# Attention kernel: the third chunk of 64 dimensions computed in full 128-row and 128-column matmul shapes

## What is computed

```python
# layer 0
q = heads(x @ W_q); k_t, v_t = heads(text @ W_k), heads(text @ W_v)        # 1020 text tokens
probs_t = softmax(q @ k_t.T * scale); text_out = probs_t @ v_t
k_ip, v_ip = heads(ip @ W_k_ip), heads(ip @ W_v_ip)                        # the last 4 tokens
sem = l2norm(probs_t @ text) @ l2norm(ip).T
ip_out = (softmax(q @ k_ip.T * scale + 0.5 * sem) * mask) @ v_ip
x = (text_out + ip_out) @ W_out + b_out + x
# layer 1: 77 text tokens and 947 ip tokens, each with its own softmax
q = split(x @ Wq.T); out = attend(q, text @ Wk.T, text @ Wv.T) + attend(q, ip @ Wk_ip.T, ip @ Wv_ip.T)
x = out @ Wo.T + bo + x
```

## Time and profile before

| | |
|---|---|
| three timed runs | 3520.0, 3520.13, 3522.02 us; median 3520.13 us |
| the profiled execution | span 3517.6 us, from first to last instruction; the profile gives no other time of it |
| PE | busy 3406.7 us, 97% of the span, 24832 matmuls |
| PEld | busy 2900.3 us, 82% |
| DVE | busy 2044.4 us, 58% |
| ACT | busy 1845.3 us, 52% |
| POOL | busy 1095.2 us, 31% |
| granted TensorE clock | 0.990 of 2.4 GHz on the mean |

### The profile page before, as it was taken

The page is one execution under the profiler, slowest core; times in us unless marked ns, Lnnn a source line. Parts: engine busy times, 40 slices in busy tenths (PEclk is TensorE's granted clock), DMA queues, the critical chain, the costliest instruction groups (busy, mean ns, idle before and its releaser), DMA issues.

```text
span 3517.6 us, 65886 instructions
## 1 busy us (share of the span) xinstructions
PE 3406.7 (97%) x24832; PEld 2900.3 (82%) x24832; DVE 2044.4 (58%) x5565; ACT 1845.3 (52%) x4030; POOL 1095.2 (31%) x932
## 2 busy tenths in 40 slices
PE   6999999999999999999999999999999999999978
PEld 4888978887888888888888878888788888889755
DVE  4444445556555565665656556656566656565678
ACT  2333333556454555555655555555555556565757
POOL 2111010234332332233333232333423322222467
PEclk8999999999999999999999999999999999999989
DMA  5433822233348333233356423324335532222233
GB/s 183 107 77 64 104 82 74 70 88 83 82 83 76 93 75 83 76 100 84 94 76 71 97 71 76 80 74 107 86 74 78 69 61 62 55 55 53 52 78 64
DMA packets 659087, 282.78 MB, mean 80 GB/s; under 512 B 481010, under 2 KB 609730, under 8 KB 658772
## 3 DMA queue, kind: packets, MB, share of 16 engines
q1 hardware_dynamic: 658772, 278.57, 38.2%
HBM read 199.44 MB, written 79.04 MB: 79 GB/s over the span
## 4 chain that ended last, share of the span: by engine, by line
PE 88%; DVE 6%; ACT 2%; issue 1%; POOL 1%; SPq 1%; DMA 1%; POOLq 0%; DVEq 0%; ACTq 0%
PE acc L1095 9%; PE acc L1088 9%; PE acc L1090 8%; PE acc L1091 8%; PE acc L1096 8%; PE acc L1089 7%; PE score L1055 4%; PE score L1139 4%; PE spare L1139 4%; PE score L1057 3%; PE av L1126 3%; PE av L1130 3%; PE score L1176 2%; PE spare L1176 2%; PE score L1225 2%; PE spare L1225 2%
## 5 line engine op out<-in xcount | busy, mean ns | idle before, releaser
L1298 ACT ACTIVATE prob<-score 128x512 f32<-128x512 f32 x1219 | 729.3, 598 | 1252.5 <-PE score L1057 1244.4
L1698 POOL TENSOR_TENSOR prob_lo<-prob,prob_hi 128x512 fp32r<-128x512 f32 x624 | 816.1, 1312 | 1525.5 <-ACT prob_hi L1301 1524.9
L1088 PE MATMUL acc<-tok_v,prob_hi 128*128 128x300 f32 x2240 | 904.1, 404 | 0.9 <-issue 0.9
L1090 PE MATMUL acc<-tok_lo,prob_hi 128*128 128x256 f32 (+1 forms) x2560 | 755.5, 295 | 0.0
L1095 PE MATMUL acc<-tok_v,prob_lo 128*128 128x278 f32 (+1 forms) x2560 | 745.8, 291 | 0.0
L1301 ACT ACTIVATE prob_hi<-score 128x512 fp32r<-128x512 f32 x1219 | 726.0, 596 | 0.0
L1091 PE MATMUL acc<-tok_lo,prob_hi 128*128 128x256 f32 (+1 forms) x2560 | 719.5, 281 | 0.0
L1096 PE MATMUL acc<-tok_v,prob_lo 128*128 128x256 f32 (+1 forms) x2560 | 717.7, 280 | 0.0
L1089 PE MATMUL acc<-tok_v,prob_hi 128*128 128x256 f32 x2240 | 627.4, 280 | 0.0
L1090 PEld LDWEIGHTS acc<-tok_lo,prob_hi 128*128 128x128 f32 (+1 forms) x2560 | 484.2, 189 | 9.1 <-issue 7.2
L1091 PEld LDWEIGHTS acc<-tok_lo,prob_hi 128*128 128x128 f32 (+1 forms) x2560 | 483.6, 189 | 6.3 <-issue 1.0
(11 more groups left out here) (325 smaller groups left out, 5141.1 us busy)
## 6 DMA issues: line engine op xcount, KB each, us to landing
k_ring<-k_scr SPq DMA_DIRECT2D x160, 384.0 KB
tok_v<-v_scr SPq DMA_DIRECT2D x158, 176.0 KB, 3.3
v_ring<-v_scr SPq DMA_DIRECT2D x160, 148.5 KB, 3.4
ctx_t<-in_ctxT SPq DMA_DIRECT2D x16, 1024.0 KB, 9.1
q_ring<-q_scr SPq DMA_DIRECT2D x160, 96.0 KB
v_scr<-v_stage SPq DMA_DIRECT2D x32, 440.0 KB, 2.6
v_scr<-v_stage SPq DMA_DIRECT2D x36, 330.0 KB, 9.6
tok_stage<-in_ctx SPq DMA_DIRECT2D x32, 256.0 KB, 2.9
```

The source lines that it names most:

```text
L1088: e.matmul(out_a[:, 0:SEG + VCOLS], p_hi, tok_v[0:kk, c, seg, v_lo:v_lo + SEG + VCOLS], start=first, stop=False)
L1090: e.matmul(out_a[:, t0:t0 + SEG], p_hi, tok_lo[0:kk, c, seg * SEG:(seg + 1) * SEG], start=False, stop=False)
L1298: e.activation(prob[:, es, :], bank_s[:, :], ACT.Exp, scale=SCALE)
L1698: e.tensor_tensor(prob_lo[:, ps, :], prob[:, es, :], prob_hi.bitcast(F32)[:, ps, :], ALU.subtract).then_inc(s_low[1], 1)
```

## The change

In all four places the third chunk is computed at full size.
- The four operands of the two projections, `w_q`, `x_in`, `w_o` and `o_t`, get 64 rows of zeros in their third chunk, written once at the start by eight memsets at the head of DVE's program. All query and finish matmuls then contract over 128 rows. Their number of columns stays `MW[m]`.
- Keys and turns of m = 2 use the last 128 output channels (192 to 319) as columns in place of the last 64. The wanted 64 channels then stand in PSUM rows 64 to 127, the other rows repeat channels of m = 1 and are not used.
- So for m = 2 the turned rows are copied from and into rows 64 to 127, `w_o`'s third chunk is loaded there, and its zeros lie in rows 0 to 63. The keys are split on all 128 rows and stored from rows 64 to 127. `edge` is as before.
- PE waits for the zeros ahead of the first query and the first finish step (`s_pad`).

```diff
+        s_pad = sem("unused_rows_zeroed")
+        HALF = P - MW[NM - 1]
+        low_rows, high_rows = slice(0, MW[NM - 1]), slice(HALF, P)
+        def rows_of_chunks(name, x):
+            return [x[:, 0:NM - 1, :], x[high_rows if name == "wo" else low_rows, NM - 1, :]]
+        def columns_to_rows(m):
+            return slice(P * m, P * m + P) if m < NM - 1 else slice(D - P, D)
+        def rows_in_psum(m):
+            return slice(0, P) if m < NM - 1 else high_rows
+        def rows_of_split(key):
+            return slice(0, P if key[0] == "k" else MW[key[2]])
...
 # PE, q
+                            if u == 0:
+                                e.wait_ge(s_pad, 4)
-  mm = e.matmul(bank[bank_of["q", u, m]][0:w, 0:SQ], w_q[wj][0:MW[k], k, P * m:P * m + w], x_in[xj][0:MW[k], k, :],
+  mm = e.matmul(bank[bank_of["q", u, m]][0:w, 0:SQ], w_q[wj][:, k, P * m:P * m + w], x_in[xj][:, k, :],
 # PE, k
-  mm = e.matmul(bank[bank_of[key]][0:w, lo:hi], (w_ip if layer else w_text)[:, k, P * m:P * m + w], ctx_t[:, k, t0 + lo:t0 + hi],
+  mm = e.matmul(bank[bank_of[key]][:, lo:hi], (w_ip if layer else w_text)[:, k, columns_to_rows(m)], ctx_t[:, k, t0 + lo:t0 + hi],
 # PE, turn
-  fl = [attn[:, st, :, :].rearrange("p h d -> p (h d)")[:, P * m:P * m + w] for st in range(ST)]
+  fl = [attn[:, st, :, :].rearrange("p h d -> p (h d)")[:, cols] for st in range(ST)]
-  e.matmul(bg[0:w, 0:SQ], v_block[:, batch_of(u) % 2, P * m:P * m + w], probs_t, start=True, stop=True)
+  e.matmul(bg[:, 0:SQ], v_block[:, batch_of(u) % 2, cols], probs_t, start=True, stop=True)
-  mm = e.matmul(bg[0:w, st * P:(st + 1) * P], fl[st], ident[:], start=False, stop=True, skip_group_check=True)
+  mm = e.matmul(bg[:, st * P:(st + 1) * P], fl[st], ident[:], start=False, stop=True, skip_group_check=True)
 # PE, finish
+                        if u == 0:
+                            e.wait_ge(s_pad, 8)
-  mm = e.matmul(bank[bank_of[key]][0:w, 0:SQ], w_o[wj][0:MW[k], k, P * m:P * m + w], o_t[oj][0:MW[k], k, :],
+  mm = e.matmul(bank[bank_of[key]][0:w, 0:SQ], w_o[wj][:, k, P * m:P * m + w], o_t[oj][:, k, :],
 # DVE, ahead of all steps
+            for x in (*w_q, *x_in):
+                e.memset(x.bitcast(F32)[high_rows, NM - 1, :], 0.0).then_inc(s_pad, 1)
+            for x in (*w_o, *o_t):
+                e.memset(x.bitcast(F32)[low_rows, NM - 1, :], 0.0).then_inc(s_pad, 1)
...
 # DVE, turn
+  w, key = rows_in_psum(m), ("turn", u, m)
-  e.tensor_copy(o_t[0][0:w, m, :], turned).then_inc(s_turned, 1)
+  e.tensor_copy(o_t[0][w, m, :], turned).then_inc(s_turned, 1)
 # DVE, split (split_hi and lower in the same way, on DVE and POOL)
-  e.tensor_copy(f, bank[bank_of[key]][0:w, lo:hi]).then_inc(s_free, 1)
+  w, (lo, hi) = rows_of_split(key), columns_of(key)
+  e.tensor_copy(f, bank[bank_of[key]][w, lo:hi]).then_inc(s_free, 1)
 # SP
-  e.dma_start(w_o_raw[0:MW[m], m, :], a[f"wo{UNITS[u][0]}"][P * m:P * m + MW[m], :]).then_inc(s_wo, 16)
+  e.dma_start(w_o_raw[rows_in_psum(m), m, :], a[f"wo{UNITS[u][0]}"][P * m:P * m + MW[m], :]).then_inc(s_wo, 16)
+  w = rows_in_psum(m) if key[0] == "k" else slice(0, n_rows)
-  part_bf[0:w, i % 2, 0:hi - lo, c0:c1]).then_inc(s_part[i % 2], 16)
+  part_bf[w, i % 2, 0:hi - lo, c0:c1]).then_inc(s_part[i % 2], 16)
```

More of the change, by code:

```diff
@@ L1166, in _ @@
                     _, u, m, half, k = s
-                    layer, w, t0 = UNITS[u][0], MW[m], 512 * half
+                    layer, t0 = UNITS[u][0], 512 * half
                     key = ("k", u, m, half)
@@ L1330, in _ @@
                         e.wait_ge(s_bg, note[s] + 1)
-                    for h, f in zip(rows_of_chunks(hi), rows_of_chunks(raw)):
+                    for h, f in zip(rows_of_chunks(name, hi), rows_of_chunks(name, raw)):
                         e.activation(h, f, ACT.Copy).then_inc(s_hi[name], 1)
@@ L1405, in _ @@
                     _, u, m, key, i = s
-                    w, (lo, hi) = MW[m], columns_of(key)
-                    f = part_f[0:w, i % 2, lo:hi]
+                    w, (lo, hi) = rows_of_split(key), columns_of(key)
+                    f = part_f[w, i % 2, lo:hi]
                     e.wait_ge(s_bg, job[key] + 1)
@@ L1410, in _ @@
                         e.wait_ge(s_part[i % 2], part_waits[i])
[L1411 removed]
+                    e.tensor_copy(f, bank[bank_of[key]][w, lo:hi]).then_inc(s_free, 1)
                 elif kind == "split_hi":
                     _, u, m, key, i = s
[L1414 removed]
+                    w, (lo, hi) = rows_of_split(key), columns_of(key)
                     e.wait_ge(*out_of_psum[job[key]])
[L1416 removed]
+                    e.tensor_copy(part_bf[w, i % 2, 0, lo:hi], part_f[w, i % 2, lo:hi]).then_inc(s_h0, 1)
                 elif kind == "lower":
                     _, u, m, key, i = s
[L1419 removed]
+                    w, (lo, hi) = rows_of_split(key), columns_of(key)
                     e.wait_ge(s_r, i + 1)
[L1421 removed]
+                    e.tensor_copy(part_bf[w, i % 2, 1, lo:hi], part_r[w, i % 2, lo:hi]).then_inc(s_h1, 1)
                 elif kind == "ip_squares":
@@ L1669, in _ @@
                     e.wait_ge(s_hi[name], 2 * nth_of[u] + i + 1)
-                    e.tensor_tensor(rows_of_chunks(lo)[i], rows_of_chunks(raw)[i], rows_of_chunks(hi.bitcast(F32))[i], ALU.subtract).then_inc(s_lo[name], 1)
+                    e.tensor_tensor(rows_of_chunks(name, lo)[i], rows_of_chunks(name, raw)[i], rows_of_chunks(name, hi.bitcast(F32))[i], ALU.subtract).then_inc(s_lo[name], 1)
                 elif kind == "turn" and s[3] == (ST if UNITS[s[1]][0] == 0 else 0):
                     _, u, m, _ = s
-                    w, key = MW[m], ("turn", u, m)
+                    w, key = rows_in_psum(m), ("turn", u, m)
                     e.wait_ge(s_bg, job[key] + 1)
-                    turned = bank[bank_of[key]][0:w, 0:SQ]
-                    e.tensor_copy(o_t[0][0:w, m, :], turned).then_inc(s_turned, 1)
+                    turned = bank[bank_of[key]][w, 0:SQ]
+                    e.tensor_copy(o_t[0][w, m, :], turned).then_inc(s_turned, 1)
                     e.wait_ge(s_turned, turn_nth[u, m] + 1)
-                    e.tensor_tensor(o_t[1][0:w, m, :], turned, o_t[0].bitcast(F32)[0:w, m, :], ALU.subtract).then_inc(s_free, 1)
+                    e.tensor_tensor(o_t[1][w, m, :], turned, o_t[0].bitcast(F32)[w, m, :], ALU.subtract).then_inc(s_free, 1)
                 elif kind == "finish" and s[3] == NM - 1:
@@ L1701, in _ @@
                     _, u, m, key, i = s
-                    w, (lo, hi) = MW[m], columns_of(key)
+                    w, (lo, hi) = rows_of_split(key), columns_of(key)
                     e.wait_ge(s_h0, i + 1)
-                    e.tensor_tensor(part_r[0:w, i % 2, lo:hi], part_f[0:w, i % 2, lo:hi], part_bf[0:w, i % 2, 0, lo:hi],
+                    e.tensor_tensor(part_r[w, i % 2, lo:hi], part_f[w, i % 2, lo:hi], part_bf[w, i % 2, 0, lo:hi],
                                     ALU.subtract).then_inc(s_r, 1)
@@ L1707, in _ @@
                     _, u, m, key, i = s
-                    w, (lo, hi) = MW[m], columns_of(key)
+                    w, (lo, hi) = rows_of_split(key), columns_of(key)
                     e.wait_ge(s_h1, i + 1)
-                    e.tensor_tensor(part_bf[0:w, i % 2, 2, lo:hi], part_r[0:w, i % 2, lo:hi], part_bf[0:w, i % 2, 1, lo:hi],
+                    e.tensor_tensor(part_bf[w, i % 2, 2, lo:hi], part_r[w, i % 2, lo:hi], part_bf[w, i % 2, 1, lo:hi],
                                     ALU.subtract).then_inc(s_h2, 1)
@@ L1797, in _ @@
                     _, u, m, key, i = s
-                    w = MW[m]
-                    rows = slice(P * m, P * m + w)
+                    n_rows = MW[m]
+                    w = rows_in_psum(m) if key[0] == "k" else slice(0, n_rows)
+                    rows = slice(P * m, P * m + n_rows)
                     e.wait_ge(s_h2, i + 1)
```

10 lines of the change are left out of this document (4 added, 6 removed).

## The result

The changed kernel takes **3471.23 us** (median of 4 runs, 3463.5 to 3477.4), where the kernel before takes 3520.07 us (4 runs): a ratio of 0.9858, 95% interval [0.9843, 0.9874], or 48.8 us less. I had predicted 3468.3 us, with a range from 3458 to 3488 us. The profiled execution has a span of 3469.4 us and a time of 3471.23 us.

What follows compares the result with a forecast made beforehand. PE was taken to bound the kernel from 60 to 3300 us. Gains of 51.0 + 1.5 + 0.3 less 1 us for waits cut the span from 3517.6 to 3465.8 us; with 2.5 us added, 3468.3 us, range 3458 to 3488.

Steps and rivals of the forecast that it cites:

- parts 1 and 2: PE-bound stretch, 60 to 3300 us: 168 steps leaving the full shape, 55 at 0.33 and 113 at 0.29 us, save 51.0 us.
- The 64*64 steps: 28 query and finish steps in the PE-bound stretch, with no profile row, taken at the narrow price of 0.29 us each.
- The one step before 60 us: One paying step ahead of the PE-bound stretch, claimed to give 0.3 us.
- nothing streams: Leaving the full shape and coming back costs 0.38 us (rows) or 0.34 us (columns) in which PE streams nothing.
- The drain rule: Skill-page rule that changing tiling mode drains TensorE; by it fp32r steps of 128*64 would pay as well.
- Rival 3: Every narrow form is its own mode, so 64*64 steps still pay as 128*64: 8.1 us of gain fail, 3476 us; 6%.
- part 3: Added costs, all taken as hidden: longer weight loads (10.6 us if uncovered), memsets (2.2 us), POOL's wider subtractions (1.2 us).
- Rival 4: Slower: 128-column weight loads of m = 2 keys and turns come to light and the drain stays, +12.8 us, 3533 us; 2%.
- the tail: Last 218 us, where PE alone does not set the end: 15 steps worth 4.5 us, 1.5 us taken, bounds 0 and 4.5.
- part 4: What is late next: 1 us lost to growing PE waits (bounds 0 and 25), 1.5 us gained in the last 218 us.
- rival 1: PE's next wait, for a probability or a bank DVE must empty, eats half: gain 27 us, time 3493 us; 9%.
- The sum: Whole kernel: 51.0 + 1.5 + 0.3 - 1 = 51.8 us off the span, giving 3465.8 us, and a time of 3468.3 us.

## Why the prediction was right, point by point

**The counts and the price (parts 1 and 2).** 51.0 us predicted by the end of layer 0, 48.9 us measured by the starts for the changed steps. The unit prices of the earlier trace rows held to 0.01 us: 0.39 and 0.34 us with a mix behind the step, 0.28 and 0.24 us with a score. Choosing the middle between the two as followers was right: both occur, and the third follower, L1140, lies between them. What is missing lies in places I can name. Three times two key steps stand directly behind each other, so 64 steps make 61 excursions (0.9 us). One key step stands beside a wait that took its gain and 0.9 us more (1.2 us), and the turns cost 0.27 us in place of 0.29 (0.4 us). One query step lost 0.5 us to a stall beside it. The one step before 60 us comes on top (0.6 us). The 64*64 steps, which had no row, cost 0.29 us as assumed.

**The reason behind the price** was not in the prediction, and it turned out sharper than "nothing streams". A change costs 0.09 us plus the exposed load of the first weights behind it. From these two numbers the excursions follow:

| step | worked out, us | by the starts, us |
|---|---|---|
| 64*128, then a mix | 2 x 0.09 + 2 x 0.107 = 0.39 | 0.385 |
| 64*64 or 128*64 fp32, then a mix | 0.18 + 0.053 + 0.107 = 0.34 | 0.34 |
| 128*32 fp32, then a mix | 0.18 + 0.027 + 0.107 = 0.31 | 0.31 |
| one 64*64 in the middle of 128*64 | 0.18 + 2 x 0.053 = 0.29 | 0.28 |

With a score behind it the two measured prices, 0.285 and 0.243 us (medians of 24 and 31), leave at most 0.01 us for the exposed part of a bf16 load. No experiment varied that load, so it stays read, not tested. What the 0.09 us consist of is open.

**The drain rule.** The Trainium skill's page "TensorEngine Tiling (Array Packing)", Key Properties, says that a change of the tiling mode drains the engine. The 0.09 us at each change are in agreement with it. Taken for every narrow shape it does not hold: fp32r of 128*64 goes in and out at 0.12 us, and so do 96 rows and 96 columns, which the page doesn't list. Rival 3, 6%, stands refuted.

**The added costs (part 3).** All were hidden as said: the memsets (2.4 us against 2.2 estimated), the longer loads of the wide keys, POOL's wider subtractions. Rival 4 had the right ingredient in the wrong place. Weight loads do come to light, but at the changes of shape, which the change removes.

**The waits and the tail (part 4).** Idle time stayed (42.8 against 43.2 us) where I allowed 1 us more; rival 1 falls. The tail is the step that failed: I took +1.5 us, and the profiled execution lost 2.6 us, outside my bounds of 0 and 4.5. PE's work there shrank by 4.8 us as counted, and idle time grew by more than that. Of the 195 longest of the 662 pieces of the chain from 3257 us to the end DVE has 58 us, ACT 32, PE 28 and POOL 14: PE's busy time is not what sets the length of the tail. The granted clock there varies too (0.90, 0.91, 0.87 in the three windows shown). In the twelve profiled executions of kernels that do the same work the tail lies between 208 and 216 us, and not at random: it is 208.2 to 210.2 us in the four kernels where turns or projections are wholly narrow, 211.8 to 215.9 us in the eight others. Which of waits, clock and the order on DVE makes this difference stays open. I should have taken zero with bounds of 4 us to both sides.

**The sum.** The spans differ by 48.2 us where I had 51.8. The terms missed by more than that and partly cancelled: 4.1 us too much for the tail and 2.1 for the steps, 2.5 us too little for the waits (I took 1 us lost, and 1.5 us were gained), and 0.1 us elsewhere. The median of the timed runs lies 1.8 us above the span, where I took 2.5. So the forecast was 2.9 us too low. That it came so near was in part luck: when it was measured again the same kernel took 3478.58 us, 10 us above the forecast and still within the range.

## What to carry to other kernels

Price a changed matmul shape by the distance between full matmuls on both sides of it, not by its own record: here an excursion cost 0.24 to 0.39 us with 64 rows or columns, however short it was. Pad to the full shape where the padding is free in streamed columns, or put narrow matmuls of the same shape side by side, since the price is per change and not per matmul. Then look whether PE's saved time reaches the end: that of the turns has not been seen to. Where medians spread by 10 us, compare two executions start by start: the 84 steps of 64 rows gave 26.5, 26.6 and 26.9 us in three pairs of kernels.

## What the runs showed of the hardware beyond the prediction

- A change between the full shape and one of 64 rows (fp32r), or of 64 or 32 columns (plain fp32), delays the next weight load: it starts 0.21 us after the matmul before in place of at once, and 0.107, 0.055 or 0.028 us of it are then exposed for 128, 64 or 32 fp32 columns. Of a bf16 load of 128 columns at most 0.01 us show.
- 96 rows and 96 columns make no change, nor do 64 columns in fp32r (0.12 us) or in a transpose (0.13 us). Between 64 and 96 there is one row: the transposes of L1251, with 66 contraction rows, start 0.12 us after the mix (median of 125 in the changed kernel).
- In the quietest stretch the streams of PE repeat between two executions to 0.2 us in 1400 us. What the two differ by, 12 us, sits in long waits (4.7 us), in shorter stalls (4.5 us) and in the tail (2.6 us); the times of one kernel spread from 3463 to 3483 us.
